# Attention in 16 groups of 256 queries instead of 8 groups of 512, with the first pass 30 units ahead

## The chip, the cores and the metric

One core of one Trainium2 chip runs the whole program. The metric is the device time of one execution in microseconds (us), as a median of several runs. TensorE is called PE, VectorE DVE, ScalarE ACT, GpSimd POOL and SyncE SP.

## What is computed

The reference is one transformer block with layer norms behind its two halves: x is 2 batches of 1024 tokens of 512 values.

```python
def attention(x):                       # 8 heads of 8 values, no 1/sqrt(d) on the scores
    qk = (x @ Wqk_w.T + Wqk_b).reshape(b, n, 8, 8, 2)     # q and k interleaved
    v = (x @ Wv_w.T + Wv_b).reshape(b, n, 8, 8)
    attn = softmax(einsum('bhqd,bhkd->bhqk', q, k)) / 8
    return einsum('bhsl,bhlv->bhsv', attn, v).reshape(b, n, 64) @ Wo_w.T + Wo_b

def ffn(x):                             # 512 -> 1792 -> 512, int4 weights, a scale per 128 inputs
    return (silu(x @ Wg.T) * (x @ Wu.T)) @ Wd.T

x = layernorm(x + attention(x))
x = layernorm(x + ffn(x))
```

## The kernel before

**Blocks and groups.** The 2048 tokens are four blocks of 512 queries (u = 0 to 3), two for each batch. A group f is four heads of one block: 8 groups. Every group goes over its 1024 keys twice.

**First pass.** It finds each query's largest score. A unit (`first_pass` on PE, `reduce` on DVE, L1181 with its PE line L900) is a matmul of 128 queries of one head by 512 keys and a reduction of the 128x512 result to 128 maxima; there are 256 units, 32 a group. Two units in a row use the two halves of PE's rows. Three PSUM banks are a ring: unit i waits until unit i-3 was reduced. When a group's units are reduced, DVE combines the halves (L1191), POOL splits the maxima into three fp16 parts (`split_max`), PE turns them (a turn "M", L906), ACT copies them out (L721), and SP copies them by DMA into rows of `stack`, beside the queries (`max_rows`, L419), where the scores' matmul subtracts them.

**Second pass.** A step n is one tile of 128 keys of one group, 64 steps: for each of two pairs of heads PE makes the scores (L979), ACT takes exp of 128x1024 (L700), and PE multiplies by v one step later (`av`, L1008). The first pass runs ahead: 46 units stand before step 0, and each later step brings 4 more, until unit 255 in step 52. From step 53 (`DRAIN`) on there are none left. At a group's end ACT copies its sums out (`av_out`, L707), PE turns them back ("avT", L942), DVE divides (`normalise`, L1200 and L1203). When a block has all its heads, PE turns them ("attT", L947) and multiplies by Wo ("wo", L956); DVE or ACT reads the product and x gets it added (L1271). In the drain the blocks 1 and 2 have these uses one by one (`aside`). DVE's other work there is the layer norm of block 0 (L1211 to L1229) and ratios of scales (`down_ratios`, L1250 to L1259; `scale_ratios`, L1235 to L1244).

**Before step 0** PE also places q and k (`put`, L885, high and low fp16 parts, copied by `keep` on ACT) and projects the second batch (L831, L841). A table `later` hangs these pieces behind units.

**After step 63** comes the FFN: 56 tiles, periods of `gate` (L1064), `up` (L1076) and `down` (L1091) matmuls, which PE does nearly without a gap. It starts once block 0 is normalised, split and transposed by DMA (`x1_parts` on POOL, `turn_x1` on SP).

**Queues.** Each engine works in the order written. SP's is: loads, row copies of groups 0 and 1, then `place_rows(sp, 1)` (12 DMAs for batch 1's queries and keys, which wait for POOL's `second_batch_parts`), the load of x's first half (2 MB), row copies of group 2, the load of the second half, row copies of group 3, and so on.

Of the kernel before, what the change touches and what calls it, by code (L numbers as in the profile page):

```python
# [21 lines left out]
P = 128  # L22
# [7 lines left out]
TB = 512  # L30
# [9 lines left out]
NG = H // HG  # L40
STEPS = NG * KT
ALL = NB * STEPS
FG = HG * BT * 2
FIRST = NB * NG * FG
# [12 lines left out]
def build(nc, x, xT, wqkT, bqk, wvT, bv, woT, bo, gq, gs, uq, us, dq, ds, ds_next, spread, out):  # L57
    ctx = ExitStack()
    with ctx:
# [62 lines left out]
        avt = sb("avt", [P, 2, TB], F32)  # L122
        att = sb("att", [P, NB, BT, HD], F32)
        attT = sb("attT", [2 * HD, TB // 2], F32)
        rec = sb("rec", [P, BT, HG], F32)
        mxh = sb("mxh", [P, 2, HG * BT, 2], F32)
        mx = sb("mx", [P, 2, HG * BT], F32)
        mres = sb("mres", [P, HG * BT], F32)
        mp = sb("mp", [P, 2, 3 * HG * BT], F16)
        mrows = sb("mrows", [3 * HG * BT, 2, P], F16)  # L130
# [51 lines left out]
        s_kept = sem("rows_kept_in_stack0")  # L182
        s_stk1 = [sem(f"rows_in_stack1_half{jj}") for jj in range(2)]
# [10 lines left out]
        s_mld = [sem(f"max_rows_in_stack{g}") for g in range(NG)]  # L194
# [66 lines left out]
        def turns_at(n, pair):  # L261

            if pair == 0:
                return []
            f, r = divmod(n + 3, KT)
            if r == 0 and f < NB * NG:
# [5 lines left out]
            if r == 2:  # L272
# [5 lines left out]
        WO_AT = (3, 4)  # L278
        LASTF = NB * NG - 2
# [3 lines left out]
        copied = [use for use in aside if use[0] != "avT"]  # L283
        copy_count = {use: i + 1 for i, use in enumerate(copied)}

        def aside_bank(*use):
            return RING[aside.index(use) % 3]

        def aside_at(n, pair):
            return [aside[n - DRAIN]] if pair and n >= DRAIN else []  # L290
        tail = [("avT", NB * NG - 1, 0), ("attT", NB - 1, 0), ("wo", NB - 1, 0), ("wo", NB - 1, 1)]
# [40 lines left out]
        placed = [use for t in range(TH) for use in ((1, 0, t), (0, 0, t), (1, 1, t))] + [(0, 1, t) for t in range(TH)]  # L332
# [21 lines left out]
        def first_unit(n):  # L354
            u, r = divmod(n, H * BT * 2)
            g, r = divmod(r, FG)
            tt, r = divmod(r, BT * 4)
            qt, r = divmod(r, 4)
            half, jj = divmod(r, 2)
            return u, g, tt, qt, half, jj  # L360
# [19 lines left out]
        STATS_AT = {1: 2, 2: 8, 3: 15}  # L380
        RESULT_AT = [p + 6 for p in ended.values()]
# [5 lines left out]
        def _(sp):  # L387
# [18 lines left out]

            def max_rows(f):

                u, g = divmod(f, NG)
# [17 lines left out]
            max_rows(1)  # L427

# [4 lines left out]
            max_rows(2)  # L433
# [5 lines left out]
            max_rows(3)  # L439

# [9 lines left out]
            for f in range(4, NB * NG):  # L450
                max_rows(f)
                if f == 5:
# [24 lines left out]
        def _(pool):  # L477
# [27 lines left out]
            for jj in range(2):  # L505
                r = ROWS * jj + MROW
                nc.gpsimd.memset(stack[1][r:r + 3, TH * N:].bitcast(F32), MINUS_ONES).then_inc(s_fill, 1)

# [8 lines left out]
            def split_max(f):  # L517

                part = [mp[:, f % 2, :].rearrange("p (j i q) -> p i j q", j=2, i=3)[:, i, :, :] for i in range(3)]
                top = mx[:, f % 2, :].rearrange("p (j q) -> p j q", j=2)  # L520
                rest = mres[:].rearrange("p (j q) -> p j q", j=2)
# [10 lines left out]
            def second_batch_parts():  # L532

                pool.wait_ge(s_unit, 6)
                pool.wait_ge(s_put, len(placed))
                nc.gpsimd.tensor_scalar(qkf, qkf, unit[:, 1:2], None, ALU.mult).then_inc(s_scaled, 1)
# [5 lines left out]
            def load_weights(f):  # L542

                pool.wait_ge(s_mld[f % NG], 16 * 2 * (f // NG + 1))
                if f == 2:
                    for c in range(C):
                        pool.dma_start(wg[:, c, :], gq[c]).then_inc(s_gu, 16)
                if f == 3:
                    for c in range(C):
                        pool.dma_start(wu[:, c, :], uq[c]).then_inc(s_gu, 16)  # L550
                if f == 4:
                    for g in range(0, G, G // 2):
                        pool.dma_start(wd[:, g:g + G // 2, :], dq[g:g + G // 2].rearrange("g p n -> p g n"))\
                            .then_inc(s_dq, 16)

            split_max(0)
            split_max(1)
            second_batch_parts()
            pool.wait_ge(s_low, 3)
# [19 lines left out]
            def add_attention(u, t):  # L579

                n = BT * u + t
                pool.wait_ge(s_xb, u * TB // N + 1)
# [3 lines left out]
            def add_bias(b):  # L586

                pool.wait_ge(s_bo, 16)
                pool.wait_ge(s_x[b], 16)
                half = x1[:, b * N // P:(b + 1) * N // P, :]  # L590
                nc.gpsimd.tensor_tensor(half, half, bo_s.unsqueeze(1).to_broadcast([P, N // P, D]), ALU.add)\
# [854 lines left out]
```

## Time and profile before

| what | value |
|---|---|
| median of 3 runs | 528.93 us (528.42 to 530.14) |
| profiled execution, its own time | 530.17 us |
| its span | 528.2 us |
| first unit, first scores | 21.1 us, 51.6 us |
| last unit reduced, first FFN matmul | 192.1 us, 220.5 us |
| busy share of PE, DVE, ACT, POOL | 96%, 78%, 77%, 47% |

The span is what the trace holds; the execution's own time has 2 us more around it. A timeline row is: start, duration from the first start to the last end, engine and line, operation, output and input, how many instructions, and in brackets how long the engine was idle before and what ended it. A row of merged instructions ends with the last of them.

### The profile page before, as it was taken

Reading aid. Unit: us, or ns where it says so; the run is one execution under the profiler, and the core shown is the slowest. Engines: PE = TensorE matmul, PEld = TensorE weight load, DVE = VectorE, ACT = ScalarE, POOL = GpSimd, SP = SyncE. Lnnn points to the kernel's source line nnn. Section 1 sums busy time; section 2 is a strip of 40 time slices with the busy share of each in tenths; the row PEclk is TensorE's granted clock in tenths of the full one; section 3 lists DMA queues with packets and bytes.
Section 4 is the critical chain, followed back from the end, with each engine's and each line's share of the span. In section 5 each row is a group of like instructions: output and inputs, shape, how many; then the busy total and the mean of one; then the engine's idle time right before and its main releaser. Section 6 shows DMA issues by size and latency. Waiting matters only on the chain.

```text
span 528.2 us, 8092 instructions
## 1 busy us (share of the span) xinstructions
PE 505.1 (96%) x2984; PEld 194.3 (37%) x2984; DVE 414.5 (78%) x706; ACT 408.6 (77%) x562; POOL 246.9 (47%) x287
## 2 busy tenths in 40 slices
PE   9899899999999999999999999999999999999991
PEld 3222223323323222334444444444444444444440
DVE  3698999989999996378787877876666866668777
ACT  1542688999899989866888888888888888888860
POOL 9000073824100715065656569385463583642864
PEclk9999899999999999999999999999999999999997
DMA  6400007576540006310312202102000002000022
GB/s 189 163 18 7 20 21 201 186 142 136 78 70 2 2 5 159 150 50 1 60 22 40 41 1 51 30 2 80 1 0 1 0 2 79 2 1 1 0 81 79
DMA packets 29687, 28.69 MB, mean 54 GB/s; under 512 B 19408, under 2 KB 21584, under 8 KB 29392
## 3 DMA queue, kind: packets, MB, share of 16 engines
q1 hardware_dynamic: 26224, 22.14, 14.5%
q0 software_dynamic: 3424, 6.03, 6.2%
q8 instruction: 24, 0.39, 0.3%
q14 instruction: 15, 0.12, 0.1%
HBM read 24.10 MB, written 4.22 MB: 54 GB/s over the span
## 4 chain that ended last, share of the span: by engine, by line
PE 86%; DVE 8%; ACT 4%; issue 1%; POOLq 0%; DVEq 0%; POOL 0%; ACTq 0%
PE ps L1076 18%; PE ps L1064 18%; PE ps L1091 17%; PE ps L1008 9%; PE ps L979 6%; PE ps L900 6%; DVE mxh L1181 3%; PE ps L831 3%; ACT pbuf L700 2%; PE ps L991 2%; PE ps L956 2%; PE ps L885 1%; PE ps L841 1%; PE ps L1018 1%; DVE st L1211 1%
## 5 line engine op out<-in xcount | busy, mean ns | idle before, releaser
L1181 DVE TENSOR_REDUCE mxh<-ps 128x1 f32<-128x512 f32 x256 | 157.4, 682 | 9.3 <-PE ps L900 8.2
L700 ACT ACTIVATE pbuf<-ps,gamma 128x1024 f32<-128x1024 f32 x128 | 141.6, 1113 | 19.7 <-PE ps L979 14.8
L780 ACT ACTIVATE ps<-ps,ratio 128x512 f32<-128x512 f32 x168 | 106.5, 659 | 41.0 <-PE ps L1064 37.9
L1091 PE MATMUL ps<-wd,stack 128*128 128x512 f16 x448 | 131.6, 379 | 0.7 <-POOL stack L622 0.7
L1076 PE MATMUL ps<-arena,wu 128*128 128x512 f16 x448 | 115.3, 379 | 1.0 <-DVE pbuf L1325 1.0
L1341 DVE TENSOR_TENSOR ps<-ps,stack 128x512 f32<-128x512 f32 x128 | 88.1, 695 | 35.1 <-PE ps L1091 33.8
L1064 PE MATMUL ps<-arena,wg 128*128 128x512 f16 x448 | 115.5, 379 | 0.1
L786 ACT ACTIVATE ps<-ps,ratio 128x512 f32<-128x512 f32 x156 | 98.9, 659 | 6.1 <-PE ps L1076 1.6
L620 POOL CAST stack<-pbuf 128x512 f16<-128x512 f32 x56 | 34.1, 609 | 94.2 <-DVE pbuf L1325 94.2
L1341 DVE TENSOR_TENSOR ps<-ps,pbuf 128x512 f32<-128x512 f32 x80 | 55.3, 697 | 26.0 <-PE ps L1091 25.6
L1008 PE MATMUL ps<-pbuf,arena 128*32 128x256 f32 x832 | 67.3, 395 | 1.7 <-ACT avt L707 1.7
L622 POOL TENSOR_TENSOR stack<-pbuf,stack 128x512 f16<-128x512 f32 x56 | 64.8, 1157 | 4.6
L1076 PEld LDWEIGHTS ps<-arena,wu 128*128 128x128 f16 x448 | 43.6, 98 | 54.5 <-DVE pbuf L1325 3.5
L1091 PEld LDWEIGHTS ps<-wd,stack 128*128 128x128 f16 x448 | 43.7, 98 | 54.0 <-POOL stack L622 1.2
L1064 PEld LDWEIGHTS ps<-arena,wg 128*128 128x128 f16 x448 | 43.2, 98 | 54.9 <-ACT pbuf L794 1.7
L900 PE MATMUL ps<-stack 64*128 64x512 f16 x256 | 61.0, 384 | 2.4 <-DVE mxh L1181 1.9
L523 POOL CAST mp<-mx 128x16 f16<-128x16 f32 x8 | 1.6, 195 | 112.6 <-DVE mx L1191 112.6
L979 PE MATMUL ps<-stack 64*128 64x512 f16 x256 | 53.1, 389 | 1.1 <-ACT pbuf L700 1.1
L1325 DVE SCALAR_TENSOR_TENSOR pbuf<-ps,scales,pbuf 128x512 f32<-128x512 f32 x56 | 41.9, 749 | 6.9 <-PE ps L1076 6.8
L794 ACT ACTIVATE pbuf<-ps,scales 128x512 f32<-128x512 f32 x56 | 38.1, 680 | 0.2 <-PE ps L1064 0.2
L900 PEld LDWEIGHTS ps<-stack 64*128 64x128 f16 x256 | 20.6, 94 | 35.4 <-DVE mxh L1181 33.1
L979 PEld LDWEIGHTS ps<-stack 64*128 64x128 f16 x256 | 13.0, 93 | 56.0 <-issue 38.5
(111 smaller groups left out, 380.3 us busy)
## 6 DMA issues: line engine op xcount, KB each, us to landing
arena<-xT SPq DMA_DIRECT2D x16, 256.0 KB, 5.8
x<-x SPq DMA_DIRECT2D x2, 2048.0 KB, 9.7
out<-x SPq DMA_DIRECT2D x3, 1024.0 KB, 4.2
stack<-down_ratios SPq DMA_DIRECT2D x1, 2048.0 KB, 7.4
wg<-gq POOLq DMA_DIRECT2D x4, 448.0 KB, 7.3
wu<-uq POOLq DMA_DIRECT2D x4, 448.0 KB, 7.3
wd<-dq POOLq DMA_DIRECT2D x2, 896.0 KB, 11.1
pbuf<-down_ratios SPq DMA_DIRECT2D x1, 1536.0 KB, 6.4
```

Of the source, the lines that this page charges most:

```text
L622: nc.gpsimd.tensor_tensor(mparts[:, 1, t % NM, :], sg[t % 2], mparts[:, 0, t % NM, :], ALU.subtract)\
L700: nc.scalar.activation(pbuf[:, pi % 4, :].rearrange("p (a n) -> p a n", a=2), ps[:, at:at + 2, :], ACT.Exp, scale=gamma[:, n // (ALL // B) ...
L780: nc.scalar.activation(gbank[t % 2], gbank[t % 2], ACT.Copy, scale=gr[:, t % G, c:c + 1])\
L786: nc.scalar.activation(ubank[t % 2], ubank[t % 2], ACT.Copy, scale=ur[:, t % G, c:c + 1])\
L900: nc.tensor.matmul(ring_bank("first", n), qs[b][rows, k, t, qt * P:(qt + 1) * P], ks[b][rows, t, half * TB:(half + 1) * TB], start=True, s ...
L979: mm = nc.tensor.matmul(bank[at + j], ks[b][rows, t, kt * P:(kt + 1) * P], qs[b][rows, k, t, :], start=True, stop=True)
L1008: mm = nc.tensor.matmul(bank[AVB][j * VC:(j + 1) * VC, lo:hi], vst[b][:, kt, g * HG + j, :], pbuf[:, (2 * n + j // 2) % 4, (j % 2) * TB + ...
L1064: mm = nc.tensor.matmul(gbank[t % 2], wg[:, c, i * P:(i + 1) * P], x1v[blk][:, a, c, :, :], start=(c == 0 and a == 0), stop=(a == 1), skip ...
L1076: mm = nc.tensor.matmul(ubank[t % 2], wu[:, c, i * P:(i + 1) * P], x1v[blk][:, a, c, :, :], start=(c == 0 and a == 0), stop=(a == 1), skip ...
L1091: mm = nc.tensor.matmul(bank[k], mparts[:, a, t % NM, k * P:(k + 1) * P], wd[:, i, :], start=(i == 0 and a == 0), stop=(a == 1), skip_grou ...
L1181: nc.vector.tensor_reduce(mxh[:, f % 2, qh, half:half + 1], ring_bank("first", n), AX.X, ALU.max)\
L1341: nc.vector.tensor_tensor(dst, bank[k], down_row(i), ALU.mult).then_inc(s_dr[k], 1)
```

## The change

- Groups become four heads by 256 queries: 16 groups, numbered by block, head half and query half. A group has 16 units. `AHEAD` goes from 46 to 30.
- A step is two key tiles of a group, so there are still 64 steps, of the same 128x1024 exps. A pair's scores are four matmuls of 256 columns instead of two of 512.
- With 16 groups there are 16 M turns, `split_max`, `av_out` (128x256 now) and avT (two transposes instead of four), and each group's maxima reach `stack` by four DMAs instead of two.
- The first pass ends in step 56; 7 steps follow instead of 11. In these the output products are made two tiles at a time, in banks 4 and 5.
- 12 `put`s instead of 16: the last four, queries of the second block of batch 0, become 8 DMAs of SP (`place_second_half`). The pieces hang behind other units.
- SP's and POOL's lists, the bias additions and the weight loads are cut and set anew. The layer norm statistics of blocks 1 to 3 and of the results stand in other FFN periods.

```diff
-NG = H // HG
-STEPS = NG * KT
+QB = 2
+QN = TB // QB
+GROUPS = H // HG * QB
+NF = NB * GROUPS
+KS = KT // 2
+STEPS = GROUPS * KS
-FG = HG * BT * 2
+MQ = HG * QT
+FG = 2 * MQ
 AHEAD = FG + 14
...
-            f, r = divmod(n + 3, KT)
+            f, r = divmod(n + 3, KS)
...
-            f, r = divmod(n - 9, KT)
+            f, r = divmod(n - 6, KS)
...
-        DRAIN = ALL - 11
-        aside = [("attT", 1, 0), ("wo", 1, 0), ("wo", 1, 1), ("wo", 1, 2), ("avT", LASTF, 0), ("wo", 1, 3),
-                 ("attT", 2, 0), ("wo", 2, 0), ("wo", 2, 1), ("wo", 2, 2), ("wo", 2, 3)]
+        DRAIN = ALL - 7
+        ASIDE = {DRAIN: ("attT", 1, 0), DRAIN + 1: ("wo", 1, 0), DRAIN + 2: ("wo", 1, 1), DRAIN + 3: ("attT", 2, 0),
+                 DRAIN + 4: ("wo", 2, 0), DRAIN + 5: ("avT", LASTF, 0), DRAIN + 6: ("wo", 2, 1)}
...
-        placed = [use for t in range(TH) for use in ((1, 0, t), (0, 0, t), (1, 1, t))] + [(0, 1, t) for t in range(TH)]
+        placed = [use for t in range(TH) for use in ((1, 0, t), (0, 0, t), (1, 1, t))]
...
-        STATS_AT = {1: 2, 2: 8, 3: 15}
-        RESULT_AT = [p + 6 for p in ended.values()]
+        STATS_AT = {1: 5, 2: 12, 3: 19}
+        RESULT_AT = (26, 34, 48)
...
-                for jj in range(2):
-                    r = ROWS * jj + MROW
-                    sp.dma_start(qs[b][r:r + 3, k, 2 * g:2 * g + 2, :],
-                                 mrows[6 * BT * jj:6 * BT * (jj + 1), f % 2, :]).then_inc(s_mld[g], 16)
+                for c in range(HG):
+                    r, t = ROWS * (c // 2) + MROW, 2 * g + c % 2
+                    sp.dma_start(qs[b][r:r + 3, k, t, h * QN:(h + 1) * QN],
+                                 mrows[3 * QT * c:3 * QT * (c + 1), f % 2, :]).then_inc(s_mld[q4], 16)
...
             max_rows(1)
+            max_rows(2)
 
             sp.wait_ge(s_low, 3)
             sp.wait_ge(s_fill, 6)
             place_rows(sp, 1)
             sp.dma_start(x1[:, 0:8, :], x[0:8].rearrange("t p n -> p t n")).then_inc(s_x[0], 16)
-            max_rows(2)
+            max_rows(3)
+            max_rows(4)
...
-                if kt == 0 and pair == 0:
-                    pe.wait_ge(s_mld[g], 16 * 2 * (u + 1))
+                if kp == 0 and pair == 0:
+                    pe.wait_ge(s_mld[q4], 16 * HG * (u + 1))
...
+                for kk in range(2):
+                    kt = 2 * kp + kk
+                    for j in range(2):
+                        rows, t = slice(ROWS * j, ROWS * (j + 1)), 2 * g + pair
+                        mm = nc.tensor.matmul(bank[at + j][:, kk * QN:(kk + 1) * QN], ks[b][rows, t, kt * P:(kt + 1) * P],
+                                              qs[b][rows, k, t, h * QN:(h + 1) * QN], start=True, stop=True)
```

Three places in the order of the engines. The first is SP's list from the first row copies on, before:

```order
L419 DMA stack<-mrows 3x8x128 [waits ring_full,turn_read_by_act]
L419 DMA stack<-mrows 3x8x128
L351 DMA stack<-x 8x4x512 [waits stack1_filled,qk_low_ready]
L351 DMA stack<-x 8x4x512 x7
L348 DMA stack<-x 8x4x1024 x4
L432 DMA x<-x 128x8x512
L419 DMA stack<-mrows 3x8x128 [waits ring_full,turn_read_by_act]
L419 DMA stack<-mrows 3x8x128
L438 DMA x<-x 128x8x512 [waits v_transposed,rows_in_stack1_half1,rows_in_stack1_half0]
```

These are groups 1 and 2, which start in steps 8 and 16. The same stretch of the change, from group 2's row copies on:

```order
L441 DMA stack<-mrows 3x2x128 [waits ring_full,turn_read_by_act]
L441 DMA stack<-mrows 3x2x128 x3
L362 DMA stack<-x 8x4x512 [waits stack1_filled,qk_low_ready]
L362 DMA stack<-x 8x4x512 x7
L359 DMA stack<-x 8x4x1024 x4
L459 DMA x<-x 128x8x512
L441 DMA stack<-mrows 3x2x128 [waits ring_full,turn_read_by_act]
L441 DMA stack<-mrows 3x2x128 x3
L441 DMA stack<-mrows 3x2x128 [waits ring_full,turn_read_by_act]
L441 DMA stack<-mrows 3x2x128 x3
L466 DMA x<-x 128x8x512 [waits v_transposed,rows_in_stack1_half1,rows_in_stack1_half0]
```

The first row copies behind the 12 placing DMAs and the load of x are now those of group 3, which starts in step 12. The second place is PE in steps 11 and 12 of the change (L930 are units, L1009 scores, L1026 the product with v):

```order
L1009 MATMUL ps<-stack 128x256 [waits attention_normalised]
L1009 MATMUL ps<-stack 128x256 x3
L930 MATMUL ps<-stack 128x512 [waits first_pass_reduced] x2
L1026 MATMUL ps<-pbuf,arena 32x256 [waits exp_done]
L1026 MATMUL ps<-pbuf,arena 32x256 x3
L1009 MATMUL ps<-stack 128x256 [waits exp_done,max_rows_in_stack3]
L1009 MATMUL ps<-stack 128x256 x3
L930 MATMUL ps<-stack 128x512 [waits first_pass_reduced] x2
```

The scores that open step 12 wait for group 3's rows; in the kernel before step 12 lies inside group 1 and its scores wait for exps alone. The third place is DVE behind the last unit, in the change (L1233 to L1251 block 0's layer norm, L1286 attT read, L1293 a product added, L1272 to L1281 the ratios for `down`, L1257 to L1266 those for gate and up):

```order
L1243 BN_AGGR mv<-st 128x2 x3
L1286 COPY attT<-ps 128x256 [waits turn_full]
L1222 RECIPROCAL rec<-ps 128x8 [waits turn_full]
L1225 TENSOR_TENSOR att<-ps,rec 128x2x32 [waits denominators_inverted]
L1293 TENSOR_TENSOR x<-ps,x 128x512 [waits turn_full,bias_added_to_x] x2
L1251 TENSOR_SCALAR x<-x,mv,rstd 128x512 [waits ln_inverse_ready]
L1251 TENSOR_SCALAR x<-x,mv,rstd 128x512 x3
L1293 TENSOR_TENSOR x<-ps,x 128x512 [waits turn_full,bias_added_to_x] x2
L1272 TENSOR_TENSOR stack<-stack 128x112 [waits down_scales_loaded]
```

Block 1's attT was followed by the ratios for `down` before; now a division, four added tiles and block 0's layer norm stand ahead of them, and block 2's attT is read behind them.

## Rows read from the trace of the kernel before

**Rows 1.** The page, part 5: costliest group, with its idle time before.

```profile
L1181 DVE TENSOR_REDUCE mxh<-ps 128x1 f32<-128x512 f32 x256 | 157.4, 682 | 9.3 <-PE ps L900 8.2
```

**Rows 2.** Windows: stretch; busy PE, weight loads, DVE, ACT, POOL; PE clock; DMA share; GB/s.

```profile
133.00:153.40 20.40, 19.94 (x201) 6.06 (x198) 19.98 (x36) 18.33 (x18) 2.75 (x6) 1.00 0.57 91
192.10:220.50 28.40, 26.94 (x169) 7.33 (x165) 17.53 (x35) 25.96 (x26) 9.67 (x14) 1.00 0.39 113
```

**Rows 3.** Timeline: first scores of two steps in a row, inside a group.

```profile
146.88 0.39 PE L979 MATMUL ps<-stack 64*128 64x512 f16 x2
...
149.27 0.39 PE L979 MATMUL ps<-stack 64*128 64x512 f16 x2
```

**Rows 4.** Chain that ended last: the same exp of two groups in a row.

```profile
133.12 1.12 ACT pbuf L700
...
153.50 1.12 ACT pbuf L700
```

**Rows 5.** Timeline: a division at a group's edge, on DVE.

```profile
144.75 0.25 DVE L1200 RECIPROCAL rec<-ps 128x16 f32<-128x16 f32 x1
```

**Rows 6.** Timeline before step 0: one `put`, the units behind it, the first scores.

```profile
30.89 0.59 PE L885 MATMUL ps<-x,pick 128*128 128x512 f16 x2
31.42 0.39 PE L900 MATMUL ps<-stack 64*128 64x512 f16 x2
...
51.60 0.38 PE L979 MATMUL ps<-stack 64*128 64x512 f16 x2
```

**Rows 7.** Windows, columns as in rows 2: one microsecond in step 2.

```profile
58.00:59.00 1.00, 1.00 (x10) 0.13 (x4) 1.00 (x3) 0.00 (x0) 0.00 (x0) 0.50 0.00 0
```

**Rows 8.** Timeline: first scores of step 5; SP placing batch 1 and loading x.

```profile
68.31 0.39 PE L979 MATMUL ps<-stack 64*128 64x512 f16 x2
...
75.53 5.75 SPq L351 DMA_DIRECT2D stack<-x  x8
81.32 2.87 SPq L348 DMA_DIRECT2D stack<-x  x4
84.23 0.45 SPq L432 DMA_DIRECT2D x<-x  x1
```

**Rows 9.** Timeline: M turn of group 3, its row copies, POOL's wait for them.

```profile
112.91 0.24 PE L906 MATMUL ps<-ident,mp 128*48 128x128 f16 x1
...
114.04 1.49 SPq L419 DMA_DIRECT2D stack<-mrows  x2
...
117.01 1.11 POOL L550 DMA_DIRECT2D wu<-uq  x2 [5.80 <-DMA stack<-mrows]
```

**Rows 10.** DMA issues: KB each, median us to landing; the last is the load of L432.

```profile
scales<-gs SPq DMA_DIRECT2D x1, 28.0 KB, 1.9
...
bqk_s<-bqk SPq DMA_DIRECT2D x1, 0.5 KB, 5.5
...
DMA to landing us min/median/max: 10.4/10.4/10.4
```

**Rows 11.** Timeline: a product by Wo in two banks; DVE's pieces in the drain.

```profile
106.32 1.13 PE L956 MATMUL ps<-wo_s,attT 64*128 64x512 f32 x4
...
195.29 0.27 DVE L1250 TENSOR_TENSOR stack<-stack 128x112 f32<-128x112 f32 x1
...
196.83 0.68 DVE L1271 TENSOR_TENSOR x<-ps,x 128x512 f32<-128x512 f32 x1
197.43 3.05 DVE L1229 TENSOR_SCALAR x<-x,mv,rstd 128x512 f32<-128x512 f32 x4
...
202.11 0.27 DVE L1235 TENSOR_TENSOR small<-scales 128x112 f32<-128x112 f32 x1
...
205.14 0.89 DVE L1244 TENSOR_TENSOR ratio<-scales,small 128x84 f32<-128x84 f32 x1
```

**Rows 12.** One line's instructions: min, median and max ns to issue a transpose.

```profile
L447 SPq DMA_TRANSPOSE arena<-split x16: 1231/1233/1335, 200.3 to 333.5; - x16
```

More of the change, by code:

```diff
@@ L276, in turns_at, with before_in_bank @@
             return []
-        WO_AT = (3, 4)
-        LASTF = NB * NG - 2
-        DRAIN = ALL - 11
-        aside = [("attT", 1, 0), ("wo", 1, 0), ("wo", 1, 1), ("wo", 1, 2), ("avT", LASTF, 0), ("wo", 1, 3),
-                 ("attT", 2, 0), ("wo", 2, 0), ("wo", 2, 1), ("wo", 2, 2), ("wo", 2, 3)]
-        copied = [use for use in aside if use[0] != "avT"]
+        WO_AT = (4, 7)
+        LASTF = NF - 2
+        DRAIN = ALL - 7
+        ASIDE = {DRAIN: ("attT", 1, 0), DRAIN + 1: ("wo", 1, 0), DRAIN + 2: ("wo", 1, 1), DRAIN + 3: ("attT", 2, 0),
+                 DRAIN + 4: ("wo", 2, 0), DRAIN + 5: ("avT", LASTF, 0), DRAIN + 6: ("wo", 2, 1)}
+        aside = list(ASIDE.values())
+        copied = [use for use in aside for _ in range({"avT": 0, "attT": 1, "wo": 2}[use[0]])]
         copy_count = {use: i + 1 for i, use in enumerate(copied)}
         def aside_bank(*use):
-            return RING[aside.index(use) % 3]
+            return 4 if use[0] == "wo" else 7
+        def before_in_bank(*use):
+            return [other for other in aside[:aside.index(use)] if aside_bank(*other) == aside_bank(*use)][-1:]
         def aside_at(n, pair):
-            return [aside[n - DRAIN]] if pair and n >= DRAIN else []
-        tail = [("avT", NB * NG - 1, 0), ("attT", NB - 1, 0), ("wo", NB - 1, 0), ("wo", NB - 1, 1)]
+            return [ASIDE[n]] if pair and n in ASIDE else []
+        tail = [("avT", NF - 1, 0), ("attT", NB - 1, 0), ("wo", NB - 1, 0), ("wo", NB - 1, 1)]
         def in_shared_banks():
@@ L542, in load_weights @@
             def load_weights(f):
[L544 to L554, printed above, removed]
+                pool.wait_ge(s_mld[f % GROUPS], 16 * HG * (f // GROUPS + 1))
+                half, kind = (f - 4) % 2, (f - 4) // 2
+                if kind < 2:
+                    for c in range(2 * half, 2 * half + 2):
+                        pool.dma_start((wg, wu)[kind][:, c, :], (gq, uq)[kind][c]).then_inc(s_gu, 16)
+                else:
+                    own = slice(half * G // 2, (half + 1) * G // 2)
+                    pool.dma_start(wd[:, own, :], dq[own].rearrange("g p n -> p g n")).then_inc(s_dq, 16)
             split_max(0)
             split_max(1)
+            split_max(2)
             second_batch_parts()
+            split_max(3)
             pool.wait_ge(s_low, 3)
@@ L766, in _ @@
                     exps(n, pair)
-                    if pair and n and n % KT == 0:
-                        av_out(n // KT - 1)
+                    if pair and n and n % KS == 0:
+                        av_out(n // KS - 1)
                     for use in turns_at(n, pair):
@@ L952, in turn @@
                         wait_attT(pe, u)
[L953 to L957 removed]
+                    for j in range(2):
+                        rows = slice(j * HD, (j + 1) * HD)
+                        mm = nc.tensor.matmul(bank[at + j], attT[rows, k * P:(k + 1) * P], wo_s[rows, :],
+                                              start=True, stop=True)
                 mm.then_inc(s_of, 1)
```

246 lines of the change are left out of this document (128 added, 118 removed).

## The prediction

> **What bounds the kernel now.** I read the windows by stage first, then the timeline of the stages in which PE is not the one that counts. The FFN is PE's and is not touched, so what counts is when it starts: 220.5 us now. Ahead of it are three stages.
>
> Up to the first scores at 51.6 us, PE and DVE alternate. PE sets the pace where a piece hangs behind every one or two units.
>
> From there to 192.1 us DVE is the bound. In a stretch of 20.4 us in the middle it is busy 19.98 us [rows 2], nearly all of it reductions, and over the whole kernel that line waited only 9.3 us [rows 1]. A step takes 149.27 - 146.88 = 2.39 us [rows 3], four reductions of 0.60 us. PE is shown busy as long, but some of that is the modelled tail of matmuls that stand while the ring is full. Eight steps take 153.50 - 133.12 = 20.38 us [rows 4], so a group's edge costs 20.38 - 8 x 2.39 = 1.26 us. About 0.6 of it is DVE's own: the division that begins at 144.75 (0.5 us with its product) and the combining of the halves [rows 5]. The rest is PE standing behind ACT.
>
> From 192.1 to 220.5 us, 28.4 us for 11 steps, no engine is full alone: DVE works 17.5 us, PE 26.9 and ACT 26.0 [rows 2].
>
> **The change, part by part.** The sum is made against the profiled execution, 530.17 us, 1.24 us above the median of the runs.
>
> Before step 0, there are 16 units fewer, but PE hangs its pieces behind single units instead of pairs, and a pair on two row halves took no longer than one. So I count only the four missing `put`s, each 31.42 - 30.89 = 0.53 us [rows 6]: -2.1. Up to about 28 us units stood for DVE, and with fewer ahead of the pieces some of that goes: -0.4, an estimate (0 to -1). Together -2.5. The 8 DMAs that replace the `put`s are issued beside this and are wanted at unit 64, in step 8: nothing. DVE is worse used here: 30 reductions of 0.60 us are 18 us in a stage of some 28 us.
>
> That is paid for at once. The first pass needs 57 steps to run out, not 53, and while it lasts the step is DVE's: 4 x 2.39 = +9.6.
>
> The opening: steps 0 to 4 take 68.31 - 51.60 = 16.7 us [rows 6, 8], 4.8 over five plain steps. One of batch 1's two reductions (0.6 us) goes ahead of step 0, where DVE is idle. In step 2 PE ran at half clock, 0.50 [rows 7], 1.2 GHz, after it had stood waiting for those reductions; I take back the 1.2 us that this step was longer than plain. Together -1.8 (0 to -1.8).
>
> Edges: about 13 lie before step 57, against some 6.3 before. Each still has the combining, the M turn with its ACT copy, and a division; the copy of the sums and the transposes are half as big. From below an edge costs DVE's own 0.5, from above the 1.26 of now; I take 0.9, as the halved parts are about half of the waiting. 13 x 0.9 - 6.3 x 1.26 = +3.8 (-1.4 to +8.4).
>
> The drain, from the last reduction, D. DVE's layer norm statistics end as before, 3.2 us behind it (195.29 - 192.1) [rows 11]. Then DVE stands for the avT of group 13, which PE has ready at D + 5.0. What follows on DVE: division 0.5, two added tiles 1.3, layer norm of block 0 3.05, two tiles 1.3, ratios for `down` 196.83 - 195.29 = 1.5, and the read of block 2's attT 0.4: D + 13.1. PE wants that attT at D + 11.5, so it stands 1.6 us. Then the other ratios, 206.03 - 202.11 = 3.9, and two tiles, 1.3, free the banks at D + 18.3. PE's product of 1.13 us, scores, and two av around the last exp bring it to D + 22.1. Against 28.4 us that is -6.3. Work saved on PE (two banks in 1.13 us, not one by one) is part of it. Late next is block 0's transposed x: SP's four transposes wait for the ratios at D + 12.7, then a store, 4 x 1.23 us [rows 12] and a landing of some 3 us: D + 21, a microsecond to spare.
>
> The FFN I cost at nothing; the moved statistics lie on a DVE that PE does not wait for there.
>
> So far: -2.5 + 9.6 - 1.8 + 3.8 - 6.3 = +2.8.
>
> **The wait at step 12.** Group 3's rows must be in `stack` when step 12 opens. Count from the first scores of step 5, 68.31, for both kernels, since the scale of batch 1 comes to POOL at the same place of the steps. SP starts its 12 placing DMAs 7.2 us later and ends them 5.75 and 2.87 us after that, at +15.9; the load of x is issued by +16.4 [rows 8]. Only then come group 3's four copies, though its M turn is in step 9. They take 1.49 / 2 = 0.74 us each, the last starts at +18.6, and rows land 117.01 - 114.78 = 2.2 us after that [rows 9]: +20.8 if nothing holds them. Step 12 is due at 7 x 2.39 plus 1.6 for edges: +18.3. That is a wait of 2.5 us at least.
>
> They lie behind 2 MB on the same queue, though, which landed 10.4 us after its issue, at +26.3 [rows 10]. What a small DMA does behind large ones the start shows: the 0.5 KB of bqk, behind five loads of 256 KB, landed in 5.5 us, the 28 KB of gs, with nothing before it, in 1.9 [rows 10]. So I let the rows land with x. POOL's own 12 placing DMAs now come some 3.5 us later, behind a fourth `split_max`, and share the engines with x; I take +27.3. The wait is 27.3 - 18.3 = 9.0 us (from 2.5 to 10.5). Behind these scores stand all units and products on PE; DVE has three banks to reduce, then both it and ACT stand too. Nothing covers it. PE restarts from standing, and a slow clock as in rows 7 costs the 1.2 us again: +1.2.
>
> The Trainium skill, "DMA: Bandwidth & Descriptors", section "Queues, rings and completion order", has both sides: each DMA engine takes descriptors in ring order, but a DMA may use only some of the 16 rings and then does not complete in the order of issue. By the first the wait is the 9.0, by the second anything down to 2.5. The row of bqk agrees with the first.
>
> Before, the copies behind this load were group 2's, wanted in step 16, four steps later.
>
> Sum: 530.17 + 2.8 + 9.0 + 1.2 = 543.2, as a median 541.9: 542.
>
> The later groups: from M turn to landing is 117.01 - 112.91 = 4.1 us [rows 9] and two more issues, 5.6; three steps less the 1.6 that stand before the M turn are 5.6, and an edge's 0.6. I count no wait, with little to spare.
>
> **The rivals.**
>
> *Short wait.* The three-row copies overtake x on rings that are through. Then 2.5 us, half the clock's price: 528.9 + 2.8 + 2.5 + 0.6 = 535. Against it is bqk.
>
> *No wait, steps as summed.* The placing DMAs would have to be through by about +13, 2.5 us sooner than SP's 0.72 us an issue allows. 528.9 + 2.8 = 532.
>
> *PE never stands at an edge (faster).* One mechanism: rows always land in time, group 3's too, and ACT's halved copy is hidden, so each edge costs only DVE's own 0.5. Price: 3.8 falls to -1.4, and the wait to 0: 528.9 + 2.8 - 5.2 = 526.5. It decides from the point where group 3's rows land before +18.3. For it: DVE was full in mid-stage [rows 2]. Against it: SP's list.
>
> **How the numbers follow.** Long wait 0.62, short wait 0.18, no wait 0.11, no standing at edges 0.09. The time is that of the first, 542; alone it has 537 to 547. For 8 in 10 I reach down over the short wait to the case without one and leave out the fast case: 531.5 to 546.5. What this kernel's measurement can tell from no change is about 0.3%, 1.6 us. Faster holds the last case: 0.09; within it falls the lower part of the no-wait case: 0.06; slower: 0.85.
>
> **What would show it.** First scores near 49 us. PE idle for some 9 us ahead of step 12's scores, released by a DMA, with group 3's copies issued right behind the load of x, and a stretch at clock 0.50 behind. Last reduction near 201 us plus that wait and clock, FFN 22 us later. The prediction is wrong if step 12 opens without a wait, if plain steps leave 2.39 us, or if edges cost 1.5 us or nothing.

## The result and the profile after

The changed kernel takes 550.65 us (median of 5 runs, 549.75 to 551.3) against 528.93 us (528.42 to 530.14): ratio 1.0401, 95% interval 1.0382 to 1.042. It is slower, as forecast, but by 21.7 us where 13 were forecast, and 4 us above the range. The profiled execution took 549.94 us, its span is 547.9 us, 19.7 more than before.

| stretch of the trace, us | before | after | change | forecast |
|---|---|---|---|---|
| up to the first scores | 51.6 | 48.36 | -3.2 | -2.5 |
| from there to the combining behind the last unit | 140.5 | 167.2 | +26.7 | +21.8 |
| from there to the first FFN matmul | 28.4 | 25.9 | -2.6 | -6.3 |
| from there to the end of the span | 307.7 | 306.5 | -1.2 | 0 |

The forecast +21.8 is 9.6 (four steps) - 1.8 (opening) + 3.8 (edges) + 9.0 (wait) + 1.2 (clock).

The page, part 5, of the changed kernel: the reductions now waited 25.4 us, against 9.3 in [rows 1].

```profile
L1202 DVE TENSOR_REDUCE mxh<-ps 128x1 f32<-128x512 f32 x256 | 159.1, 681 | 25.4 <-PE ps L930 25.0
```

The timeline of SP, which answers to the SP rows of [rows 8]: 12 placing copies, the load of x, group 3's four row copies right behind it.

```profile
69.83 5.74 SPq L362 DMA_DIRECT2D stack<-x  x8
75.62 2.81 SPq L359 DMA_DIRECT2D stack<-x  x4
78.48 0.45 SPq L459 DMA_DIRECT2D x<-x  x1
79.04 2.98 SPq L441 DMA_DIRECT2D stack<-mrows  x4
```

The chain that ended last, at the same place (start, duration, what): the last row copy was issued at 81.3 us and was 11.38 us in flight; step 12 began when it landed.

```profile
81.32 11.38 DMA stack<-mrows
...
92.74 0.61 PE ps L1009 x4
```

The timeline of PE gives the wait, 11.57 us. The first scores of step 5 stood at 62.61 us:

```profile
62.61 0.39 PE L1009 MATMUL ps<-stack 64*128 64x256 f16 x4
...
92.74 0.61 PE L1009 MATMUL ps<-stack 64*128 64x256 f16 x4 [11.57 <-DMA stack<-mrows]
```

Windows (columns as in [rows 2]): a stretch of 40.4 us around the wait; ten microseconds of it in which no engine works while the DMA engines are 90% busy; one microsecond behind it at half clock, 0.50; and the drain, which answers to the second row of [rows 2] with PE no longer near full.

```profile
80.00:120.40 40.40, 27.02 (x288) 9.49 (x288) 26.71 (x47) 24.00 (x28) 7.77 (x19) 0.87 0.63 151
...
82.00:92.00 10.00, 0.00 (x0) 0.00 (x0) 0.00 (x0) 0.00 (x0) 0.00 (x0) 0.68 0.90 222
...
93.50:94.50 1.00, 1.00 (x10) 0.20 (x8) 0.69 (x2) 1.00 (x1) 0.00 (x0) 0.50 0.00 0
215.60:241.40 25.80, 19.56 (x213) 7.97 (x209) 18.15 (x37) 17.99 (x21) 9.57 (x14) 0.93 0.30 73
```

In the drain the ratios for `down` (L1272 to L1281), 1.5 us in the kernel before [rows 11], take 4.3 us, from 226.50 to 230.83. POOL splits the normalised x at that time (L596, L598). The timeline of DVE:

```profile
226.50 0.73 DVE L1272 TENSOR_TENSOR stack<-stack 128x112 f32<-128x112 f32 x1
227.26 0.51 DVE L1274 TENSOR_SCALAR stack<-stack 128x112 f32<-128x112 f32 x1
227.80 1.26 DVE L1277 TENSOR_TENSOR stack<-stack 128x112 f32<-128x112 f32 x1
229.10 0.50 DVE L1279 RECIPROCAL stack<-stack 128x56 f32<-128x56 f32 x1
229.63 1.20 DVE L1281 TENSOR_TENSOR stack<-stack 128x56 f32<-128x56 f32 x1
230.76 0.41 DVE L1286 COPY attT<-ps 128x256 f32<-128x256 f32 x1
```

and of POOL, in the same stretch:

```profile
227.03 0.67 POOL L596 CAST split<-x 128x512 f16<-128x512 f32 x1
227.78 1.15 POOL L598 TENSOR_TENSOR split<-x,split 128x512 f16<-128x512 f32 x1
228.88 0.65 POOL L596 CAST split<-x 128x512 f16<-128x512 f32 x1
229.61 1.15 POOL L598 TENSOR_TENSOR split<-x,split 128x512 f16<-128x512 f32 x1
```

DVE's two-input instructions of 227.80 and 229.63 us end within 0.15 us of POOL's that began beside them (228.93, 230.76). PE waited for the copy of attT that stands behind them:

```profile
231.32 1.13 PE L983 MATMUL ps<-wo_s,attT 64*128 64x512 f32 x4 [4.06 <-DVE attT L1286]
```

Block 0's transposes wait for the ratios too, and the chain that ended last goes over them: the store of the ratios, SP's four transposes (from 232.39 us) and the landing of the last one; the first FFN matmul, at 241.44 us, stood 0.60 us for it.

```profile
230.87 1.51 DMA down_ratios<-stack
...
236.52 4.79 DMA arena<-split
```

The same shows 2 us behind the opening of step 20 (115.54 us): combining the halves of the maxima, 0.17 us alone, took 1.79 us. The timeline of DVE; POOL's addition of the bias to two tiles ran from 116.88 to 119.26 us:

```profile
117.50 1.79 DVE L1212 TENSOR_TENSOR mx<-mxh 128x8 f32<-128x8 f32 x1
```

### The profile page after: what moved, and what is told of

Same layout as the page of the kernel before. It is cut to its first block, busy times and chain, and to the rows that moved or that the text cites. A ratio compares the mean times of both kernels' runs of the same rounds, so it can differ in the third digit from the quotient of the medians.

```text
span 547.9 us, 8999 instructions
## 1 busy us (share of the span) xinstructions
PE 505.7 (92%) x3336; PEld 206.4 (38%) x3336; DVE 421.9 (77%) x730; ACT 408.4 (75%) x574; POOL 255.1 (47%) x326
## 4 chain that ended last, share of the span: by engine, by line
PE 75%; DVE 12%; DMA 4%; ACT 3%; SPq 3%; issue 2%; POOL 1%; POOLq 0%; DVEq 0%; ACTq 0%
PE ps L1083 18%; PE ps L1095 17%; PE ps L1110 17%; DVE mxh L1202 6%; PE ps L1026 6%; PE ps L930 5%; PE ps L1009 4%; PE ps L859 3%; DMA stack<-mrows 3%; ACT pbuf L724 2%; PE ps L869 1%; PE ps L913 1%; SPq L362 1%; DMA arena<-split 1%; PE ps L1036 1%
## 5 line engine op out<-in xcount | busy, mean ns | idle before, releaser
L1202 DVE TENSOR_REDUCE mxh<-ps 128x1 f32<-128x512 f32 x256 | 159.1, 681 | 25.4 <-PE ps L930 25.0
L814 ACT ACTIVATE ps<-ps,ratio 128x512 f32<-128x512 f32 x156 | 98.9, 659 | 5.5 <-PE ps L1095 1.2
L1026 PE MATMUL ps<-pbuf,arena 128*32 128x256 f32 x1024 | 81.6, 396 | 0.3 <-ACT pbuf L724 0.2
L930 PE MATMUL ps<-stack 64*128 64x512 f16 x256 | 63.6, 384 | 3.3 <-DVE mxh L1202 2.9
L1009 PE MATMUL ps<-stack 64*128 64x256 f16 x512 | 51.0, 278 | 16.7 <-DMA stack<-mrows 12.0
L551 POOL CAST mp<-mx 128x8 f16<-128x8 f32 x16 | 3.1, 192 | 101.2 <-DVE mx L1212 100.8
L1009 PEld LDWEIGHTS ps<-stack 64*128 64x128 f16 x512 | 15.2, 94 | 72.2 <-issue 30.6
L1026 PEld LDWEIGHTS ps<-pbuf,arena 128*32 128x32 f32 x1024 | 21.4, 109 | 29.2 <-issue 19.2
```

What stands on the lines that cost most here:

```text
L814: nc.scalar.activation(ubank[t % 2], ubank[t % 2], ACT.Copy, scale=ur[:, t % G, c:c + 1])\
L930: nc.tensor.matmul(ring_bank("first", n), qs[b][rows, k, t, qt * P:(qt + 1) * P], ks[b][rows, t, half * TB:(half + 1) * TB], start=True, s ...
L1009: mm = nc.tensor.matmul(bank[at + j][:, kk * QN:(kk + 1) * QN], ks[b][rows, t, kt * P:(kt + 1) * P], qs[b][rows, k, t, h * QN:(h + 1) * QN ...
L1026: mm = nc.tensor.matmul(bank[AVB][j * VC:(j + 1) * VC, h * QN:(h + 1) * QN], vst[b][:, kt, g * HG + j, :], pbuf[:, (2 * n + j // 2) % 4, l ...
L1202: nc.vector.tensor_reduce(mxh[:, f % 2, qh, half:half + 1], ring_bank("first", n), AX.X, ALU.max)\
```

## The experiments

In all of them "group from step n" is the time between the first scores of steps n and n + 4. Plain ones take 10.44 us in the changed kernel; those that begin in steps 12, 16, 20, 28, 32 and 36 took 11.50, 11.30, 12.85, 11.13, 11.03 and 10.88. Every kernel is the changed one with only the edit that is shown or named. Times are medians of 4 runs, of 12 for the last two; the kernel before, in the same comparisons, had 528.85 to 529.96 us.

**1. Group 3's rows ahead of x.**

```diff
-            sp.dma_start(x1[:, 0:8, :], x[0:8].rearrange("t p n -> p t n")).then_inc(s_x[0], 16)
             max_rows(3)
+            sp.dma_start(x1[:, 0:8, :], x[0:8].rearrange("t p n -> p t n")).then_inc(s_x[0], 16)
             max_rows(4)
```

> Only the order of two issues on SP's queue changes: group 3's four row copies go ahead of the 2 MB load of x instead of behind it. Theory A (the copies are held by the load that stands ahead of them in the queue): the wait ahead of step 12's scores falls from 11.6 us to 0 to 3 us (the copies can be issued when M's copy is ready, near 79 us, and a row copy with nothing large ahead of it lands in about 2 us), and the kernel takes 540 to 543 us; up to 2 us of this may come back at step 16, whose copies then stand behind the load. Theory B (the 16 DMA engines are full with the placing copies and x, whatever the queue): the copies still land 8 us late or more, the time stays at 547 to 551 us.

544.11 us, ratio 1.0285 (1.0262 to 1.0308). The gain is 6.5 us, but the last copy was still 4.84 us in flight. The chain:

```profile
80.99 4.84 DMA stack<-mrows
```

PE stood 4.8 us ahead of step 12, between what the two theories had: moving the rows ahead of x took most of the wait, and something was left.

**2. x on another queue.** The load is issued by ACT behind step 10's exps, at 77.4 us.

```diff
+                    if (n, pair) == (10, 1):
+                        act.dma_start(x1[:, 0:8, :], x[0:8].rearrange("t p n -> p t n")).then_inc(s_x[0], 16)
```

> The load of x goes out at about the same moment (near 78 us), from ACT's queue, behind step 10's exponentials; SP's queue holds only the placing copies and then group 3's rows. Theory A (order in one queue): step 12's wait falls to 0 to 3 us, time 540 to 543 us. Theory B (the DMA engines are full at that moment): the wait stays at 8 to 11 us, since both loads are in flight together as before, time 547 to 551 us. Something between 3 and 8 us of wait would mean that queue order and load on the engines share it.

548.23 us, ratio 1.036 (1.0339 to 1.038). The chain:

```profile
80.99 9.09 DMA stack<-mrows
```

The wait is 9.1 us, as theory B has it. Theory A falls: 2 MB in flight from another queue hold the copies nearly as long, and only 2.3 us of 11.38 come from standing behind x in one queue. Experiment 1 did more than that, since there x was behind the rows and not beside them.

**3. x some 17 us later.** The load moves behind `max_rows(4)`, by the same edit as in 1, one line further.

> The first load of x goes behind group 4's row copies, some 20 us later; the placing copies of the second batch on SP's and POOL's queues stay where they are. It splits the 4.8 us by which group 3's copies were still late when they stood ahead of the load. Theory G (the placing copies alone keep the DMA engines full): the wait ahead of step 12 stays at 4.3 to 5.5 us. Theory H (the load, issued right behind, shared the engines and made them late): it falls to 2.5 us or less. The time is 543 to 545 us under G (also if the load now delays nothing else), 540 to 542 us under H.

550.89 us, ratio 1.0411 (1.0392 to 1.0431). Group 3's last copy was 4.61 us in flight, as theory G has it: the placing copies alone make that. The time was forecast wrong. The two loads of x now went out 0.6 us apart, at 95.7 and 96.2 us, and group 5's rows, issued from 103.17 us, landed at 114.1. POOL's first two loads of weights, of 448 KB each, were in flight until 108.9 us as well. The group from step 16 took 16.50 us, the next 14.02. A second wait stands eight steps later. The chain:

```profile
81.08 4.61 DMA stack<-mrows
...
103.17 1.60 SPq L441
...
106.70 7.40 DMA stack<-mrows
```

**4. Placing behind group 3's rows**, with x still ahead of group 4's.

```diff
+            max_rows(3)
             sp.wait_ge(s_low, 3)
             sp.wait_ge(s_fill, 6)
             place_rows(sp, 1)
             sp.dma_start(x1[:, 0:8, :], x[0:8].rearrange("t p n -> p t n")).then_inc(s_x[0], 16)
-            max_rows(3)
             max_rows(4)
...
             pool.wait_ge(s_low, 3)
+            pool.wait_ge(s_mld[3], 16 * HG)
             place_rows(pool, 0)
```

> The placing copies of the second batch go behind group 3's row copies: on SP's queue by order, on POOL's by a wait for those copies; the load of x stays ahead of group 4's copies. If placing and load together were the whole wait, step 12 opens 0 to 1.5 us late, no stretch at half clock follows, and the time is 537 to 539.5 us (550.65 less 11.6 us of wait and 1.1 us of clock). If the wait stays above 3 us, something other than these transfers holds the rows (the chain of M, ACT's copy and four issues of 0.72 us each on SP's queue).

546.71 us, ratio 1.0333 (1.0313 to 1.0352). Step 12 opens at 80.96 us without a wait, its last copy 1.72 us in flight. But the group from step 12 takes 19.02 us: group 4's copies now stand behind SP's 12 placing copies and x, beside POOL's 12. The added wait does its part: it holds POOL's placing until 80.7 us, and the split of group 4's maxima, which stands behind it in POOL's list, begins at 87.5 us. The chain:

```profile
78.25 1.72 DMA stack<-mrows
...
91.47 8.46 DMA stack<-mrows
```

I had priced the wait as removed, and it was moved by four steps; 3.9 us of the 12.7 of wait and clock were gained.

The flight of the last row copy, by what else is under way, orders the causes: 1.72 us with nothing large; 3.52 us with POOL's placing beside it and SP's only behind it (experiment 9); 4.61 us with both queues' placing; 9.09 us with x from ACT's queue as well; 11.38 us with x ahead of it in its own queue. So of 11.38 us some 2.9 are the placing, 4.5 x in flight beside the copies, and 2.3 its place ahead of them in one queue. The Trainium skill, "DMA: Bandwidth & Descriptors", section "Queues, rings and completion order", says that a DMA engine takes turns between the queues it has work for, a packet each. In kind experiment 2 agrees: with x on ACT's queue alone the copies on SP's queue took 9.09 us, and 4.61 us without x. The size is no test of the rule, since POOL's queue had work too.

**5. POOL's additions in its wait.** `add_bias` and `add_attention` go ahead of `load_weights(f)` in POOL's list.

```diff
                 split_max(f)
-                if 4 <= f < 10:
-                    load_weights(f)
                 for i in {5: (0,), 6: (1,), 9: (2,), 10: (3, 4), 11: (5, 6), 12: (7,)}.get(f, ()):
                     add_bias(i)
                 for t in {7: (0, 1), 8: (2, 3)}.get(f, ()):
                     add_attention(0, t)
+                if 4 <= f < 10:
+                    load_weights(f)
```

> Only the order on POOL within a group changes: the additions of the bias and of the attention output to x come before the weight loads, so in the time in which POOL otherwise waits for the group's rows, and no longer when the next group's maxima are combined. Theory C (those additions, running beside the end of a group, slow DVE's combine from 0.17 to 0.8 us and delay the split of the maxima): the groups from step 28 to step 44 fall from 10.9 to 11.1 us to 10.44 us, the one from step 20 gets shorter by 1 us or more, the kernel gains 2.5 to 4 us, 546.5 to 548 us. Theory D (the weight loads' traffic or the ring's reductions make those groups longer): groups keep 10.9 us or more and the time stays within 0.3% of 550.65 us.

549.05 us, ratio 1.0371 (1.0349 to 1.0393). The intervals of the two ratios overlap; the trace tells the kernels apart. One line's instructions, min/median/max ns of the combining: at most 168, where the changed kernel had 1792. The groups from steps 28, 32 and 36 fall to 10.43, 10.43 and 10.44 us: 1.7 us in all, less than the 2.5 I gave at least. The group from step 20 keeps 12.68 us, so that part of theory C was wrong: the chain there runs through ACT's copies of output products.

```profile
L1212 DVE TENSOR_TENSOR mx<-mxh x16: 166/168/168, 33.8 to 214.9; 128x8 f32<-128x8 f32 x16
```

In this profile the wait ahead of step 12 was 12.0 us and the group behind it took 12.58 us instead of 11.50, which hides most of the gain in its span. Over that group the granted clock was 0.76, against 0.86 in the changed kernel's profile: it stood at 0.50 until 98.9 us here and until 95.9 us there. Why it lasted longer is not known.

**6. The ratios for `down` early.**

```diff
             att_out(1)
+            down_ratios()
             normalise(LASTF - 1)
...
-            down_ratios()
             att_out(2)
```

> Only down_ratios (seven small DVE operations) moves in the drain: to right behind att_out(1), ahead of POOL's split of x1, which it ran beside. Theory E (it took 4.3 us only because POOL worked beside it, and the copy of attT(2), the output products and so the last additions stood behind it): down_ratios takes about 1.5 us again, PE's 4.1 us wait ahead of wo(2,0) falls below 2 us, from the last reduction to the first gate 22 to 23.5 us instead of 25.9, time 547 to 548.5 us. Theory F (the drain is bound by the transposes of x1 and by POOL's parts, whatever DVE does): down_ratios may get shorter, the drain stays at 25 us or more and the time within 0.3% of 550.65 us.

545.71 us, ratio 1.0308 (1.0284 to 1.0332). The drain takes 20.2 us instead of 25.9, better than theory E's 22 to 23.5. Its clock is 1.00, against 0.93 of the changed kernel, where PE had stood 4.06 us, so some of the gain is the clock's. The median gains 4.9 us; as in experiment 5, the profile has a wait of 12.0 us ahead of step 12 and 12.61 us for the group behind it. The same five instructions take 1.6 us, on the timeline of DVE:

```profile
220.43 0.26 DVE L1272 TENSOR_TENSOR stack<-stack 128x112 f32<-128x112 f32 x1
220.73 0.22 DVE L1274 TENSOR_SCALAR stack<-stack 128x112 f32<-128x112 f32 x1
220.98 0.28 DVE L1277 TENSOR_TENSOR stack<-stack 128x112 f32<-128x112 f32 x1
221.29 0.50 DVE L1279 RECIPROCAL stack<-stack 128x56 f32<-128x56 f32 x1
221.83 0.22 DVE L1281 TENSOR_TENSOR stack<-stack 128x56 f32<-128x56 f32 x1
```

The ratios for gate and up, which now run beside POOL's split in their place, go from 2.0 to 4.0 us, two input instructions first (L1261, 0.28 to 1.26 us). The Trainium skill, "SBUF — State Buffer", section "Who interferes with whom", says that VectorE and GpSimd share a pair of ports, that an instruction of VectorE with two inputs in SBUF waits there for the whole of a GpSimd instruction that reads SBUF and began first, and that `tensor_reduce` never does. The traces agree for POOL's additions and its split: the combining ended with POOL's addition, and the reductions, mean 681 ns, are as long as in [rows 1]. The page also lets a `tensor_scalar` wait; L1274 took 0.51 us beside the split and 0.22 in its new place. But not every POOL instruction does it. In that new place POOL's reciprocal root of 128x4 ran beside the ratios, and L1277, with two inputs, still took 0.28 us inside it. The timeline of POOL:

```profile
220.60 1.05 POOL L542 TENSOR_TENSOR rstd<-veps,mhalf 128x4 f32<-128x4 f32 x1
```

**7. All orders together.** Experiments 4, 5 and 6, and x in four loads of 1 MB behind the row copies of groups 3 to 6.

> All orders together: placing behind group 3's rows, x in four loads of 1 MB, each behind a group's row copies, POOL's additions ahead of its weight loads, down_ratios behind att_out(1). If the causes add up: 550.65 less 12.7 (wait and clock), less 1.8 (groups on POOL's side), less 4.2 (drain), less 0.5 to 1 (group 5's rows behind the second load) is 531 to 532 us, 0.3 to 0.7% above the kernel before. Rival: the causes hide behind each other (the split loads meet the weight loads, or a new wait opens at group 4 or 6), and it stays at 534 us or more.

535.13 us, ratio 1.0116 (1.0091 to 1.014): the rival, a new wait at group 4. The groups from step 24 on are plain, the drain 20.2 us, but the one from step 12 still takes 16.53 us. The chain shows why: POOL, held by my own wait for group 3's rows, issues its 12 placing copies from 81.03 to 87.80 us, ahead of the split of group 4's maxima, and group 4's rows then fly 5.92 us behind them and x.

```profile
81.86 3.79 POOL stack L362 x7
85.66 2.14 POOL stack L359 x4
87.80 0.21 POOL mp L558
...
91.84 5.92 DMA stack<-mrows
```

**8. Placing and loads spread.** POOL places where it did, and x goes in four loads of 1 MB (`load_x`) behind the row copies of groups 5 to 8. SP's list (`place_rows` now takes the kinds to place, 0 Q rows, 1 K rows), with experiment 5:

```diff
+            max_rows(3)
             sp.wait_ge(s_low, 3)
             sp.wait_ge(s_fill, 6)
-            place_rows(sp, 1)
-            sp.dma_start(x1[:, 0:8, :], x[0:8].rearrange("t p n -> p t n")).then_inc(s_x[0], 16)
-            max_rows(3)
+            place_rows(sp, 1, (0,))
             max_rows(4)
+            place_rows(sp, 1, (1,))
...
                 max_rows(f)
+                if f < 9:
+                    load_x(f - 5)
...
-                for i in {5: (0,), 6: (1,), 9: (2,), 10: (3, 4), 11: (5, 6), 12: (7,)}.get(f, ()):
+                for i in {6: (0, 1), 9: (2,), 10: (3, 4), 11: (5, 6), 12: (7,)}.get(f, ()):
```

> Placing and loading are spread so that no group's rows stand behind them: on SP's queue group 3's rows, the eight copies of Q rows, group 4's rows, the four copies of K rows, and x in four loads of 1 MB behind the rows of groups 5 to 8; POOL places where it did, and its additions go ahead of its weight loads. If the 12.7 us of wait and clock and the 1.8 us on POOL's side really go away and come back nowhere: steps 12 and 16 open within 1 us of their time, every group from step 12 takes 10.4 to 11 us (12.7 for the one with the first output products), and the time is 535 to 537.5 us. Rival: the transfers have nowhere to go without delaying some group's rows (a wait of 3 us or more at step 16, 20 or 24), time over 539 us.

> The kernel of the run beside it with down_ratios behind att_out(1). If the drain's loss is independent of the waits, it gains another 4 to 5 us, as it did alone: 530.5 to 533 us, 0.3 to 0.8% above the kernel before. Rival: the drain gains less than 2 us since it now starts elsewhere.

> The same, with scale_ratios (five DVE operations, 4.0 us beside POOL's split of x1) behind the first two additions of the third output product instead of ahead of them, since the second half of that product waits for the banks that these additions read. If that wait bounds the drain: 1 to 2 us less than the run beside it, 529 to 531.5 us, about the time of the kernel before. Rival: the drain is bound elsewhere or the ratios come late for the first scaling: the same time or more.

| kernel | median, us | ratio (interval) | step 12 opens | group from step 24 | drain |
|---|---|---|---|---|---|
| spread | 543.95 | 1.0284 (1.0242 to 1.0327) | 82.14 | 16.68 | 26.1 |
| and `down_ratios` early | 536.91 | 1.014 (1.0115 to 1.0164) | 82.11 | 16.35 | 20.2 |
| and `scale_ratios` late | 536.43 | 1.0133 (1.0111 to 1.0155) | 82.52 | 17.28 | 19.5 |

All three lie above what was expected of them. The waits ahead of steps 12 and 16 are gone: step 12 opens 1 us late, step 16 10.3 us behind it. A new loss of 6 us stands between steps 24 and 28, which no theory had: ahead of the M turn of group 7 (126.14 us in the second kernel) PE is idle for 4.83 us, and restarts at half clock. It was of my making: the addition to the first two tiles of x waited for the semaphore of two loads, so for a load issued at 114.11 us. POOL stood 11.8 us, and group 7's maxima, combined by 119.1 us, were split from 124.96 us on. The timeline of POOL, second of the three kernels:

```profile
119.28 4.65 POOL L625 TENSOR_TENSOR x<-x,wqk_s 128x1024 f32<-128x1024 f32 x2 [11.80 <-DMA x<-x]
123.87 1.10 POOL L583 DMA_DIRECT2D wu<-uq  x2
124.96 0.21 POOL L557 CAST mp<-mx 128x8 f16<-128x8 f32 x1
```

The late `scale_ratios` shortened the drain by 0.7 us; its time does not tell it from the run beside it.

**9. The same, mended.** A semaphore for each load of x, and SP's wait for the placed rows behind group 5's copies. The second kernel also moves an output product of block 0 by one step (`WO_AT = (4, 8)`).

```diff
-        s_x = [sem(f"x_loaded{b}") for b in range(B)]
+        s_x = [sem(f"x_loaded{b}") for b in range(4)]
...
-                pool.wait_ge(s_x[i // BT], 16)
+                pool.wait_ge(s_x[i // 2], 16)
...
                 max_rows(f)
+                if f == 5:
+                    for jj in range(2):
+                        sp.wait_ge(s_stk1[jj], 16 * PARTS)
+                    sp.wait_ge(s_vt, B)
```

> The kernel with all orders (and the late scale_ratios), in which the first addition to x waits for its own 1 MB load alone instead of for two (it stood on POOL until 119.3 us and delayed the split of group 7's maxima), and in which SP waits for the placed rows behind group 5's row copies instead of ahead of them. If that wait was the 6 us between step 24 and step 28: 536.43 less 6 less 1 is 529 to 530.5 us, the time of the kernel before within 0.3%, which accounts for the whole of the 21.7 us. Rival: a transfer of x or of weights then delays another group's rows by 2 us or more, 532 us or above.

> The run beside it with the second output product of the first block one step later, at step 24 instead of 23, so that ACT copies the two products (1.0 us each) in different groups. If ACT's copies make the group from step 20 2.2 us longer than the plain 10.44: that group falls to 11 to 11.7 us, the next rises by 0.5 us at most, 0.5 to 1.5 us less in all, 528 to 529.5 us. Rival: the group is long for another reason, or the next takes over the loss: no change.

529.21 us (528.67 to 529.72), ratio 0.9996 (0.9985 to 1.0008), and 529.74 us, ratio 1.0001 (0.9991 to 1.0012). The 21.7 us are gone; with other orders and semaphores, and x in four loads for two, the new tiling stands level with the kernel before. The groups from step 12 on take 10.32, 10.92, 12.67, 10.32 and then 10.44 us. Moving the output product only moved the loss: 12.67 and 10.32 became 11.77 and 11.79, 0.6 us more in all, where 0.5 to 1.5 us less was expected. The chain and, in a fence of its own, two windows of the first kernel:

```profile
77.83 3.52 DMA stack<-mrows
```

```profile
80.00:120.40 40.40, 37.90 (x421) 13.58 (x420) 36.69 (x69) 35.03 (x39) 13.24 (x27) 1.00 0.57 133
200.80:220.20 19.40, 17.78 (x213) 7.69 (x209) 16.29 (x37) 17.11 (x19) 9.57 (x14) 1.00 0.39 88
```

The changed kernel's row of the same 40.4 us (first of its windows above) has PE busy 27.02 us at a clock of 0.87, with 151 GB/s moved; here it is 37.90 us at full clock, with 133 GB/s. What cost the time was when the transfers ran, far more than how many.

## Why the prediction was right and wrong

**Right.** The mechanism of the likeliest case and its place: a wait ahead of step 12, ended by group 3's rows, which stood behind the load of x. SP's placing began 7.2 us behind step 5's scores, as said, and the load's issue ended 16.3 us behind them (+16.4 forecast). Step 12 was due at +18.6 (+18.3). A plain group takes 10.44 us; 4 x 2.39 + 0.9 is 10.46. Without its wait and its slow clock the stretch of steps rose by 14.0 us, and 9.6 - 1.8 + 3.8 = 11.6 was forecast. The clock behind the wait cost 1.1 us (the group from step 12 took 11.50 us, not 10.44); 1.2 was the forecast.

**Wrong in size, four terms.** Against the profiled execution the forecast lacks 549.94 - 543.2 = 6.7 us.

*The wait, 9.0 forecast, 11.6 measured (+2.6).* The step that failed is "POOL's own 12 placing DMAs [...] share the engines with x; I take +27.3": they landed at +30.1. I gave 1.0 us to the sharing (26.3 to 27.3) and took the flight of x, 10.4 us, from a row in which POOL's placing had been issued 1.6 us before x went out; here it was issued until 2.3 us after that, and x took 14.3 us. The upper bound of 10.5 us, for which the prediction shows no working, was too low. The reason that I gave, one queue's order, was the smaller part: 2.3 us of the flight, as experiment 2 shows.

*The drain, -6.3 forecast, -2.6 measured (+3.7).* The failing term is "ratios for `down` 196.83 - 195.29 = 1.5". That row was read beside POOL's 128x4 instruction alone, and the change had moved the work beside POOL's split of x, where it took 4.3 us. The order stood in the prediction, and so did the warning: the other ratios, read beside POOL, cost 3.9 us for as many instructions, and I did not ask why. The path that ended last was the one with "a microsecond to spare", over the transposes: their landing came 25.8 us behind the last reduction, where 21 was forecast. The ratios ended 2.6 us late; the rest is the store (1.5 us, some 0.4 in the sum) and a last transpose that landed 4.8 us behind its issue, where issue and landing had been put at some 4.2. Experiment 6, which moved both paths forward, took back 5.7 us.

*The edges (+2.4 with the opening).* 1.7 of it are the groups from steps 28, 32 and 36, in which POOL's additions stood in its list behind a wait for the group's rows and ran when the next combining and split were due. "The later groups [...] I count no wait" did not look at POOL. Another 0.9 is the group from step 16, 11.30 us: group 5's rows were 3.07 us in flight, with the second load of x ahead of them, and PE stood 0.43 us for them at step 20. So that sentence failed there for the rows too. In experiment 9, without that wait, the group still took 10.92 us; where this half comes from is open.

*Ahead and behind.* The first scores came 0.7 us earlier than forecast, and the FFN was 1.2 us shorter; no run here separates its moved statistics from the rest. The last 2 us are no stretch of the trace: the profiled execution lay 1.24 us above the median before and 0.71 below it after.

**The rivals.** The rows did not overtake x: with its 2 MB ahead in the queue they were 11.38 us in flight, and 8.46 us in experiment 4. The fast case fell with its first condition. Its cheap edges did not come either: a plain group takes 10.44 us in the changed kernel and in the mended one, an edge of 0.9 us and not of 0.5. Against the kernel before, the mended one gives back 3.8 us ahead of the steps, 9.0 in the drain (28.4 to 19.5) and 1.2 in the FFN, and loses 12.5 in the steps (153.0 us from the first scores to the last combining, against 140.5), in all 1.5 us less of span: too little for its time to show.

## What to carry to other kernels

In these kernels a small copy that opens a stage came late whenever large ones or many others were in flight, on whatever queue: move them behind it, and then look at the next small copy, since each transfer that is moved meets one (experiments 3, 4 and 7). A duration read from a trace belongs to the neighbours that it had there: where a change moves two-input VectorE work next to GpSimd work, price it from a row in which both run. An engine that waits in order should do its other work inside that wait, and a wait should name the one transfer that it needs.

## What the runs showed of the hardware beyond that

- Busy DMA engines need not move much. Windows of experiment 3: with placing copies alone the share is 0.77 at 127 GB/s, with the two loads of x 0.86 at 290. And group 3's row copy was in flight until 85.69 us, though no transfer of any queue began from 84.5 us on (a window counts transfers that begin in it): its last microsecond was not a matter of full engines. Which engines these copies use was not looked at.

```profile
80.00:83.00 3.00, 1.28 (x18) 0.45 (x14) 2.06 (x4) 1.55 (x2) 0.90 (x2) 1.00 0.77 127
83.00:86.00 3.00, 0.26 (x4) 0.20 (x6) 0.00 (x0) 0.00 (x0) 0.00 (x0) 0.55 0.07 4
84.50:86.00 1.50, 0.26 (x4) 0.20 (x6) 0.00 (x0) 0.00 (x0) 0.00 (x0) 0.50 0.00 0
...
97.00:102.00 5.00, 5.00 (x58) 1.83 (x56) 4.97 (x10) 4.61 (x6) 1.87 (x6) 1.00 0.86 290
```

- DVE's 128x8 combining, both inputs in SBUF, took 0.17 us alone and up to 1.79 us beside a POOL addition, ending with it; beside POOL's 128x4 instruction of 1.05 us a two-input one of 128x112 took 0.28 us. A reciprocal of 128x56, one input, took 0.50 us in both places.
- After 11.6 us of standing TensorE restarted at 0.50 of its clock, 1.2 GHz. The groups behind waits of 11.6 and 12.0 us took 11.50 and 12.58 us, at granted clocks of 0.86 and 0.76, where a plain one takes 10.44. The 4.8 us of standing in experiment 1 cost as much as the 11.6: the group behind it took 11.42 us at 0.87.
